# A depthwise convolution over four tokens, folded into its projection as four shifted TensorE products

## The reference, cut to what matters

```python
x_and_gate = x @ W_in + b_in
x_ssm, gate = jnp.split(x_and_gate, 2, axis=-1)
# depthwise, causal: token t sees x_ssm of t-3 .. t, zeros ahead of the sequence
xc = conv(x_ssm, conv_w, padding=[(3, 0)]) + conv_b
x_conv = silu(xc)
B_mat, C_mat = jnp.split(x_conv @ W_x + b_x, 2, axis=-1)
# scan: h = A_discrete * h + xc_t * B_t ;  y = C_t . h + D * xc_t
y = (y * silu(gate)) @ W_out + b_out
```

## Time and profile before

| | |
|---|---|
| time, median of 3 runs | 664.75 (663.4 to 666.9) |
| the profiled execution, its own time | 668.37 |
| its span, first to last instruction | 666.6 |
| TensorE matmul busy | 532.3 (80%) |
| VectorE busy | 534.1 (80%) |
| GpSimd busy | 351.4 (53%) |
| ScalarE busy | 291.3 (44%) |
| mean granted TensorE clock | 0.947 of full |
| chain that ended last | VectorE 45%, TensorE 26%, issue 17%, ScalarE 8% |

### The profile page before, as it was taken

The page is one execution under the profiler, slowest core; times in us unless marked ns, Lnnn a source line. Parts: engine busy times, 40 slices in busy tenths (PEclk is TensorE's granted clock), DMA queues, the critical chain, the costliest instruction groups (busy, mean ns, idle before and its releaser), DMA issues.

```text
span 666.6 us, 6051 instructions
## 1 busy us (share of the span) xinstructions
PE 532.3 (80%) x1784; PEld 313.3 (47%) x1795; DVE 534.1 (80%) x827; ACT 291.3 (44%) x470; POOL 351.4 (53%) x283
## 2 busy tenths in 40 slices
PE   2248886797988998897898988889889887677774
PEld 1236664464645664465446554656456433323331
DVE  3631251499889998998989998999699979998965
ACT  3235566454643565364534644456525631222110
POOL 1624552487438663774546764675476644433333
PEclk9988998998998999997998999899989998779969
DMA  8200000000000000000000000000000000000000
GB/s 325 81 2 0 18 0 1 16 0 1 0 17 0 33 0 16 1 32 1 16 1 31 2 0 1 16 17 0 0 1 16 1 0 0 16 1 0 16 0 16
DMA packets 5505, 11.63 MB, mean 17 GB/s; under 512 B 736, under 2 KB 1504, under 8 KB 5216
## 3 DMA queue, kind: packets, MB, share of 16 engines
q1 hardware_dynamic: 4464, 9.47, 3.9%
q10 hardware_dynamic: 1008, 1.77, 0.8%
HBM read 9.13 MB, written 2.10 MB: 17 GB/s over the span
## 4 chain that ended last, share of the span: by engine, by line
DVE 45%; PE 26%; issue 17%; ACT 8%; POOL 1%; DMA 1%; DVEq 1%; SPq 0%; POOLq 0%; ACTq 0%
DVE xbank L1119 9%; PE bank0a L755 9%; DVE hs L1132 8%; PE bank1a L837 4%; DVE plain L1010 3%; PE ybank L861 3%; DVE xn L981 2%; DVE yn L1036 2%; DVE beats L1094 2%; DVE beats L1092 2%; ACT plain L512 1%; DVE tie L1089 1%; DVE beats L1096 1%; PE bank0a L713 1%; PE bank1a L811 1%
## 5 line engine op out<-in xcount | busy, mean ns | idle before, releaser
L439 POOL TENSOR_TENSOR pr<-hs,Ct 128x512 f32<-128x512 f32 x128 | 173.8, 1358 | 156.8 <-DVE hs L1132 142.2
L861 PE MATMUL ybank<-pr,gat 128*128 128x512 f32 x256 | 136.8, 617 | 5.6 <-POOL pr L439 5.1
L853 PE MATMUL xbank<-xpair,spr 128*128 128x512 f32 x128 | 95.6, 747 | 17.3 <-DVE hs L1132 17.1
L427 POOL TENSOR_TENSOR hidAl<-plain,hidAh 128x512 fp32r<-128x512 f32 x48 | 63.8, 1330 | 62.8 <-ACT hidAh L513 52.1
L1119 DVE TENSOR_TENSOR xbank<-xbank,Bt 128x512 f32<-128x512 f32 x128 | 87.8, 686 | 5.9 <-PE xbank L853 5.7
L427 POOL TENSOR_TENSOR hidBl<-plain,hidBh 128x512 fp32r<-128x512 f32 x48 | 63.1, 1316 | 46.9 <-ACT hidBh L513 42.4
L1132 DVE TENSOR_TENSOR_SCAN hs<-decay,carry,xbank 128x512 f32<-128x512 f32 x64 | 81.7, 1276 | 7.1
L1132 DVE TENSOR_TENSOR_SCAN hs<-decay,xbank 128x512 f32<-128x512 f32 x64 | 77.8, 1215 | 6.3
L861 PEld LDWEIGHTS ybank<-pr,gat 128*128 128x128 f32 x256 | 48.4, 198 | 40.6 <-issue 21.3
L755 PE MATMUL bank0a<-hidAh,hTh 128*128 128x512 f32 x128 | 56.5, 442 | 8.1 <-ACT hidBh L513 7.3
L755 PE MATMUL bank0a<-hidBh,hTh 128*128 128x512 f32 x128 | 58.6, 458 | 1.1 <-ACT hidAh L513 0.8
(11 more groups left out here) (145 smaller groups left out, 1045.5 us busy)
## 6 DMA issues: line engine op xcount, KB each, us to landing
xt<-x_tok SPq DMA_DIRECT2D x8, 256.0 KB, 2.7
xr<-x_feat SPq DMA_DIRECT2D x8, 256.0 KB, 8.1
out<-xr SPq DMA_DIRECT2D x8, 256.0 KB, 2.0
fh<-h_w SPq DMA_DIRECT2D x1, 1024.0 KB, 11.2
pr<-h_w SPq DMA_DIRECT2D x1, 1024.0 KB, 13.5
lw<-l_w ACTq DMA_DIRECT2D x1, 640.0 KB, 7.4
g<-spread ACTq DMA_DIRECT2D x1, 512.0 KB, 6.5
Bt<-w_in SPq DMA_DIRECT2D x1, 512.0 KB, 8.9
```

The source lines that it names most:

```text
L427: pool.tensor_tensor(low[:, m, :], plain[:, k % NPLAIN, :], high[:, m, :].bitcast(F32), ALU.subtract).then_inc(hidden_low, 1)
L439: pool.tensor_tensor(pr[:, i % NPR, :], hs[:, i % NHS, :], Ct[:, hs_(u)], ALU.mult).then_inc(p_ready, 1)
L853: pe.matmul(xbank[i % 2][:], spr[:, at, :], xpair[:, half, hs_(u)], start=True, stop=True).then_inc(xs_full, 1)
L861: pe.matmul(ybank[:], gat[:, P - DPG * (k + 1):2 * P - DPG * (k + 1)], pr[:, i % NPR, :], start=(k == 0), stop=(k == NGRP - 1)).then_inc(y ...
```

## The change

The convolution is linear, so the four taps go into the weights: `w_conv[:, k, :]` is the first half of W_in with its columns scaled by tap k, and four products of the layer-normed input `ynT`, each shifted by one more token, add up in `bank1a`. In the second half of a sequence three narrow products bring in the last tokens of the half before; in the first half one product with the identity takes away the bias that the padding must not have (`b_edge`). ScalarE's silu reads the bank, with the combined bias `b_conv`. VectorE's four steps, the eviction of `ssm` and its buffer go. The score projection moves from slot 7 to slot 6; taps 3 and 2 are issued in slot 7 and taps 1 and 0 in slot 8. On ScalarE `convolved` moves to slot 9 and the gate to slot 10, as in `L1_ACT`; on TensorE the gate's product stays in slot 9. At the start, one more DMA (256 KB), one product on GpSimd (the weights) and six tiny operations on VectorE (the biases) are added.

```diff
-        L1_ACT += [(_k, _n) for _k in ("xnT", "ssm", "score", "gate", "B", "C")]
+        L1_ACT += [(_k, _n) for _k in ("xnT", "score", "conv", "gate", "B", "C")]
...
+            pool.wait_ge(l1_params, 16 * NPARAM_L1)
+            pool.tensor_tensor(w_conv[:], lw[:, 0:P].rearrange("p (o d) -> p o d", o=1).broadcast_to([P, TAPS, P]),
+                               raw_conv, ALU.mult).then_inc(w_conv_ready, 1)
...
@@ -477,7 +483,8 @@
         def _(act):
             act.dma_start(mask[:], decay_mask).then_inc(params, 16)
             act.dma_start(grow[:], gamma_row).then_inc(params, 16)
-            for dst, src in ((raw_spr, spread), (lw[:], l1_w), (gat[:], gather), (tri[:], before_mask), (w2l[:], w2_l1)):
+            for dst, src in ((raw_spr, spread), (lw[:], l1_w), (gat[:], gather), (tri[:], before_mask), (w2l[:], w2_l1),
+                             (gate[:, 0:TAPS * P], conv_rows)):
                 act.dma_start(dst, src).then_inc(l1_params, 16)
...
-            def take_ssm(t):
-                if t > 0:
-
-                    act.wait_ge(conv_step, t * TAPS)
-                at = TAPS - 1 + t % 2 * HALF
-                take1(("ssm", t), ssm[:, at:at + HALF], ACT.Identity, bias=scale("b_in"))
-
...
             def take_gate(t):
+                take1(("gate", t), gate[:, hs_(t)], ACT.Silu, bias=scale("b_in", 1))
+
+            def convolved(t):
+                if t == 0:
+                    act.wait_ge(b_conv_step, 5)
+                    act.wait_ge(w_conv_ready, 1)
                 if t >= 2:
+
                     act.wait_ge(yg_ready, t - 1)
-                take1(("gate", t), gate[:, hs_(t)], ACT.Silu, bias=scale("b_in", 1))
-
-            def convolved(t):
-                act.wait_ge(conv_step, (t + 1) * TAPS)
-                act.activation(xc[:, hs_(t)], cv[(TAPS - 1) % 2][:, hs_(t)], ACT.Silu,
-                               bias=scale("conv_b")).then_inc(xc_ready, 1)
-                act.wait_ge(xc_ready, t + 1)
+                take1(("conv", t), xc[:, hs_(t)], ACT.Silu, bias=b_conv[:, 0:1])
+                act.wait_ge(l1_act_done, done(L1_ACT, ("conv", t)))
                 for half in range(2):
                     rows = slice(half * P // 2, (half + 1) * P // 2)
                     last = act.activation(xpair[rows, half, hs_(t)], xc[rows, hs_(t)], ACT.Copy)
                 last.then_inc(x_high, 1)
 
             def take_B(t):
+                if t >= 2:
+
+                    act.wait_ge(xs_done, step(t - 1, 0))
                 take1(("B", t), Bt[:, hs_(t)], ACT.Identity, bias=scale("b_x", 0))
...
@@ -637,9 +640,9 @@
                         retention_q(w)
                 if n is not None:
                     if k == 9:
+                        convolved(n)
+                    elif k == 10:
                         take_gate(n)
-                    elif k == 10:
-                        convolved(n)
                     elif k == 11:
                         take_B(n)
...
+                def convolve(t, taps):
+
+                    if TAPS - 1 in taps:
+                        open1a(("conv", t))
+                        pe.wait_ge(l1_act_done, done(L1_ACT, ("xnT", t)))
+                        if t == 0:
+                            pe.wait_ge(w_conv_ready, 1)
+                            pe.wait_ge(b_conv_step, 5)
+                    for k in taps:
+                        s = TAPS - 1 - k
+                        if s > 0 and t % 2 == 1:
+                            pe.matmul(bank1a[:, 0:s], w_conv[:, k, :], ynT[:, (t - 1) % NYNT, HALF - s:HALF],
+                                      start=False, stop=False)
+                        last = pe.matmul(bank1a[:, s:HALF], w_conv[:, k, :], ynT[:, t % NYNT, 0:HALF - s],
+                                         start=(s == 0), stop=(k == 0))
+                        if s == 0 and t % 2 == 0:
+                            pe.matmul(bank1a[:, 0:TAPS - 1], ident[:], b_edge[:], start=False, stop=False)
+                    if 0 in taps:
+                        last.then_inc(l1_act_full, 1)
...
@@ -881,9 +904,11 @@
                         elif k == 5:
                             norm_to_features(n)
                         elif k == 6:
-                            project("ssm", n, W_IN[:, 0:P])
+                            project("score", n, W_R)
                         elif k == 7:
-                            project("score", n, W_R)
+                            convolve(n, (3, 2))
+                        elif k == 8:
+                            convolve(n, (1, 0))
...
-            def convolve(t, k):
-
-                at = t % 2 * HALF + k
-                if k == 0:
-                    dve.wait_ge(l1_act_done, done(L1_ACT, ("ssm", t)))
-                    dve.wait_ge(pad_ready, 1)
-                    dve.tensor_scalar(cv[0][:, hs_(t)], ssm[:, at:at + HALF], scale("conv_w", 0), None,
-                                      ALU.mult).then_inc(conv_step, 1)
-                else:
-                    dve.wait_ge(conv_step, t * TAPS + k)
-                    dve.scalar_tensor_tensor(cv[k % 2][:, hs_(t)], ssm[:, at:at + HALF], scale("conv_w", k),
-                                             cv[(k + 1) % 2][:, hs_(t)], ALU.mult, ALU.add).then_inc(conv_step, 1)
+            def conv_biases():
+
+                dve.tensor_scalar(b_taps[:], col[:, COLS["conv_w"]], scale("b_in"), -1.0, ALU.mult,
+                                  ALU.mult).then_inc(b_conv_step, 1)
+                dve.wait_ge(b_conv_step, 1)
+                dve.tensor_copy(b_edge[:, 2:3], b_taps[:, 0:1]).then_inc(b_conv_step, 1)
+                dve.wait_ge(b_conv_step, 2)
+                for k in (1, 2):
+                    dve.tensor_tensor(b_edge[:, 2 - k:3 - k], b_edge[:, 3 - k:4 - k], b_taps[:, k:k + 1],
+                                      ALU.add).then_inc(b_conv_step, 1)
+                    dve.wait_ge(b_conv_step, 2 + k)
+                dve.tensor_tensor(b_taps[:, 3:4], b_edge[:, 0:1], b_taps[:, 3:4], ALU.add).then_inc(b_taps_summed, 1)
+                dve.wait_ge(b_taps_summed, 1)
+                dve.tensor_tensor(b_conv[:], scale("conv_b"), b_taps[:, 3:4], ALU.subtract).then_inc(b_conv_step, 1)
...
@@ -1156,8 +1183,6 @@
                     stats_l0(w)
                 if n is not None and k == 2:
                     stats_l1(n)
-                if n is not None and 8 <= k < 10:
-                    convolve(n, 2 * (k - 8))
                 if u is not None:
                     scan(u, k)
                 if last is not None and k == 1:
@@ -1172,8 +1197,6 @@
                     output(last)
                 if w is not None and k == 6:
                     norm_l0(w)
-                if n is not None and 8 <= k < 10:
-                    convolve(n, 2 * (k - 8) + 1)
```

More of the change, by code:

```diff
@@ L167, in program @@
         spr = sb("spr", [P, NGRP // 2, P], F32R)
+        w_conv = sb("w_conv", [P, TAPS, P])
+        b_taps = sb("b_taps", [P, TAPS])
+        b_edge = sb("b_edge", [P, TAPS - 1])
+        b_conv = sb("b_conv", [P, 1])
         gat = sb("gat", [P, 2 * P - DPG])
@@ L226, in program @@
         yg = Bt
-        cv = [Bt, xc]
         Ct = sb("Ct", [P, SEQ])
@@ L249, in program @@
         consts_set = sem("consts_set")
-        pad_ready = sem("pad_ready")
+        w_conv_ready = sem("w_conv_ready")
+        b_conv_step = sem("b_conv_step")
+        b_taps_summed = sem("b_taps_summed")
         theta_ready = sem("theta_ready")
@@ L328, in program @@
         raw_spr = g1[:, 0:NGRP // 2 * P]
+        raw_conv = gate[:, 0:TAPS * P].rearrange("p (k d) -> p k d", k=TAPS)
         FFN_WEIGHTS = [(raw_w12, w12h[:].rearrange("p a n -> p (a n)"), w12l[:].rearrange("p a n -> p (a n)"))]
@@ L1233, in _ @@
             dve.wait_ge(decay_ready, 1)
+            conv_biases()
             for p in PERIODS:
```

13 lines of the change are left out of this document (4 added, 9 removed).

## The result

| | before | after |
|---|---|---|
| time, median (lowest to highest), 4 runs each on one chip | 664.08 (661.67 to 666.9) | 675.37 (674.0 to 675.67) |
| after / before, 95% interval | | 1.0162 [1.0132, 1.0192] |
| profiled execution, its span | 668.37, 666.6 | 675.1, 673.3 |
| mean granted TensorE clock | 0.947 | 0.970 |
| VectorE busy | 534.1 | 507.9 |

What follows compares the result with a forecast made beforehand. The prediction took VectorE and TensorE to hand each other the critical path at the convolution. Start and period terms summed to +15.5 us, clock falls added 4.3, total +19.8: 664.75 + 19.8 = 684.5 us, range 672 to 693.

Steps and rivals of the forecast that it cites:

- What bounds the kernel: Slot 11: VectorE bounds odd periods, with 1.26 us of TensorE slack in u=1; TensorE bounds even ones.
- The wait at the gate: Slot 9: TensorE's gate product waits 2.8 us for the convolution's silu in periods -1 to 4, about 1.0 in u=5.
- Rival A: Not slower: ScalarE evicts the convolution early enough that the gate doesn't stall; -0.4, or 664 us; chance 8%.
- 5 x 2.8 + 1.0 + 0.9: Stall time that rival A would remove: five periods at 2.8 us, u=5 at 1.0, period -1 at 0.9.
- The products: TensorE ahead of slot 9: three more full products at 0.86 us, narrow ones at 0.22; 2.80 odd, 3.24 even periods.
- The periods: Change of each period up to slot 11's times_b, from added products, stall, vanished waits and slack; VectorE carries it on.
- The odd periods: u=1 and u=3: 2.80 products + 2.8 stall - 0.39 - 1.26 slack = +3.95 us each.
- 0.39 for a wait that goes: u=1 and u=3: 0.39 us subtracted because a wait for the scan goes.
- nearly free: u=6: TensorE nearly free, VectorE gains 3.05 us, less 0.3 for later scores: -2.7.
- The start: Start-up: one more GpSimd weight product delays VectorE's subtraction, which TensorE awaits: +1.3 us.
- The clock: After five stalls in u=0 to u=4: half followed by a clock fall at 1.7 us, +4.3; ends 0 and 14.
- stalls half as long: Low end of the range, 672 us: 15.5 - 7, with no clock fall.

Runs made afterwards that it cites:

- second profile of before: Kernel before the change, profiled once more with no code changed; 665.74 us, one run.
- second profile of after: Changed kernel, profiled once more with no code changed; 673.2 us, one run.
- third profile of before: Kernel before the change, profiled a third time with no code changed; 663.38 us, one run.

## Why the prediction was right, and where it was off

**What bounds the kernel** was read rightly for slots 8 to 11. VectorE's saving did not count in u=0 to u=5: the waits for `xbank` at slot 11 are there in all six, 2.2 to 5.3 us where 2 to 4 was forecast, and putting the steps back into the changed kernel cost 4.5 to 7 us instead of 21. The waits at score_column in the even periods are gone, as forecast. That VectorE carries every delay from slot 11 on undiminished held in the changed kernel, whose `times_b` never waits in slots 12 to 15. With the stall gone it doesn't hold: the odd periods had the same length with and without the steps, with waits in slot 15.

**The wait at the gate** was forecast at 2.8 and is 2.69, in periods -1 to 4. In u=5 I expected 1.0; it is 0.59 there, but `times_b` waits 2.69, 1.12 and 2.19 in slots 9 to 11, and the period is 2.8 longer (68.6 against 65.8), as forecast. Part of that is luck: slots 8 to 10 are 2.6 longer, and a fall of the clock that stands ahead of them before and behind them after takes 1.5 off and puts 1.7 on. Rival A's cure is now measured: the silu ahead of the query's eviction gives 660.5, the gate's product in slot 10 659.3. The term of "5 x 2.8 + 1.0 + 0.9" = 15.9 us for the stalls is borne out by the moved product, 16. The moved silu gained 15 while 0.8 us of each wait stayed, so it does not measure that term by itself.

The Trainium skill ("ScalarE: Activation LUTs", What ACT_TABLE_LOAD costs) gives, as an estimate from its drain of about 1.38 us, 4.2 for each stall. The trace of after disagrees again, and this time at both ends of the load: it begins 0.02 us after the query's eviction (234.63 + 0.60, then 235.25), and the silu 0.01 after the load.

**The products.** 0.86 for a full one is right. The narrow ones were taken at 0.22 and take 0.14, by TensorE's timeline in period -1 of after, whose narrow product starts at 93.69 and the next one at 93.83; it shows as one row:

```profile
93.69 0.28 PE L832 MATMUL bank1a<-b_edge,ident 128*128 128x3 f32 x2
```

**The periods.** Against the second profile of before, the changed kernel's first one has

| | period -1 | u=0 | u=1 | u=2 | u=3 | u=4 | u=5 | u=6 | u=7 |
|---|---|---|---|---|---|---|---|---|---|
| forecast | +2.8 | +0.6 | +3.95 | -0.5 | +3.95 | +3.3 | +2.8 | -2.7 | 0 |
| measured | +2.6 | +0.5 | +2.9 | +0.6 | +4.3 | +2.4 | +2.8 | -3.9 | -2.9 |

(period -1 worked out as the first `times_b` less the start of TensorE's main part, 127.59 - 37.38 against 124.93 - 37.32.) The odd periods were taken too long by 1.1 each. Behind a stall with no fall of the clock u=1 and u=3 take 72.0, so +2.9 and, by the second profile of after, +2.8; the 4.3 of u=3 above has a fall of 1.5 in it. Only a small part of the 1.1 is clock. In u=1 before has a fall ahead of slot 8, and after has none. But the third profile of before has full clock in u=3, and with it slots 0 to 7 are 1.0 shorter and slots 8 to 10 0.7 longer, so that the period loses 0.3 (68.9 against 69.2). The term itself is too large then: 3.1 at full clock in both kernels, not 3.95. Which part of it is too large was not separated; its 0.39 for a wait that goes stands in none of the rows that it names. The second and third 8 us of u=1, of before and of after:

```profile
204.00:212.00 8.00, 5.85 (x20) 3.69 (x19) 7.79 (x18) 3.04 (x5) 6.24 (x6) 0.88 0.00 0
212.00:220.00 8.00, 8.00 (x36) 5.96 (x36) 7.70 (x12) 4.04 (x6) 3.98 (x4) 0.91 0.00 0
```

```profile
204.00:212.00 8.00, 5.88 (x24) 3.52 (x23) 7.79 (x18) 2.82 (x5) 6.32 (x6) 1.00 0.00 0
212.00:220.00 8.00, 8.00 (x38) 5.76 (x38) 7.70 (x12) 4.38 (x7) 5.52 (x5) 1.00 0.00 0
```

In u=6 slots 8 to 10 are 2.75 us shorter, as forecast; the other 1.18 is clock. The windows are slots 8 to 10 and the rest of the period, of before, of its third profile and of after:

```profile
569.93:582.42 12.49, 8.39 (x21) 4.13 (x20) 12.36 (x17) 3.94 (x9) 5.83 (x4) 0.73 0.00 1
582.42:603.98 21.56, 16.96 (x37) 6.62 (x37) 19.74 (x30) 7.71 (x15) 6.52 (x5) 0.84 0.00 1
```

```profile
567.31:579.80 12.49, 8.37 (x20) 4.10 (x19) 12.36 (x17) 3.93 (x9) 5.83 (x4) 0.73 0.00 1
579.80:600.18 20.38, 14.97 (x37) 5.65 (x36) 19.65 (x29) 6.79 (x15) 5.62 (x5) 1.00 0.00 1
```

```profile
583.51:593.25 9.74, 9.74 (x34) 5.03 (x32) 8.96 (x13) 4.39 (x9) 5.11 (x4) 1.00 0.00 1
593.25:613.63 20.38, 13.65 (x34) 4.92 (x33) 19.64 (x29) 6.44 (x13) 5.61 (x5) 1.00 0.00 0
```

12.49 becomes 9.74, whatever the clock; 21.56 is 20.38 wherever the clock stays up, in the kernel before too. With the steps kept in the changed kernel it is 12.49 and 21.56 again, with 1.00 and 0.84 granted. That TensorE is "nearly free" in u=6 isn't borne out: without taps 1 and 0 slots 8 to 10 take 8.42, so the two products weigh 1.3 there, and what the steps had cost there is 4.1 (12.49 - 8.42), not 3.05. The 2.7 came out right because the two errors nearly cancel.

**The start** was the first term that failed: "+1.3" is 0, since the weight product came after the subtraction that it was to delay, and the 4.95 us of the earlier trace rows was one of two lengths that this subtraction has.

**The clock** was the second, and with the odd periods the one that matters: "I take half of them at 1.7: +4.3". For the falls behind the stalls that is not far off: of the five in u=0 to u=4 two were followed by a fall in the first profile of after and one in the second, at 1.3 to 1.6 us each. But it is only half of the account, and the whole has the other sign. TensorE's mean clock went from 0.947 to 0.970. Over the span that is 2 x 0.053 x 666.6 = 71 us at half speed before and 2 x 0.030 x 673.3 = 40 us after. Falls behind the new stalls exist: after that of period -1 the clock is 0.50, by the window of the changed kernel

```profile
104.00:110.00 6.00, 6.00 (x12) 4.13 (x13) 1.37 (x2) 2.35 (x4) 0.00 (x0) 0.50 0.00 0
```

and the gate's product at 103.98 takes 2.08 instead of 1.13. But I counted only falls that come, and none of those that go: of u=6's last slots (1.2) and of u=7's (2.9).

The terms that differ from the forecast, with u=2 and u=3 at their lengths without a fall (72.5 and 72.0): start -1.3, periods -1 to 5 -3.9, of which the odd u=1 and u=3 are 2.2 and u=4 0.9, falls behind the stalls 3.1 instead of 4.3, falls that go -4.1. Together that is -10.5, and 19.8 less these is 9.3, where the two profiles are 661.9 - 652.5 = 9.4 apart. So the direction and the stall were forecast rightly, and the time lies in the range, but not for the reason that the range's low end was drawn from: "stalls half as long". The stalls were whole.

## What to carry to other kernels

When work moves between engines, look at each in-order queue that a new result passes through: here one eviction behind another made TensorE wait 2.7 us six times, and the same convolution is 1.6% slower than before with that wait and 0.9 to 1.6% faster with the gate's product moved out of it. Ask it of each queue in turn; the same move of the gate's product that cured the changed kernel cost the old one 28 us, because there the gate led ScalarE's run and here the convolution does. A saving on an engine that waits afterwards is no gain, but once the wait is taken away, part of it can be had.
